# Q from an already turned x, small operations in PSUM, and x turned by DMA before a quantized feed-forward, on one core

## The reference

```python
x = x + xattn(layernorm(x), ctx, ctx, wq, wk, wv, wo)
x = x + ffn(layernorm(x), W_in, b_in, W_out, b_out)
# xattn, 16 heads of 16 features:
corr = irfft(rfft(Q) * conj(rfft(K)))        # along the 128 positions, for each feature
top_vals, top_idx = top_k(corr, 4)
w = softmax(top_vals)
out = sum_i w_i * (V rolled by top_idx_i inside its head)   # then @ wo
# ffn, 1024 hidden features, everything rounded to integers first:
x_q = round(x * 32767 / max|x|);  W_q = round(W * 127 / max|W|)   # one maximum over all of x
hidden = gelu(x_q @ W_in_q + b_in)
out = round(hidden * 32767 / max|hidden|) @ W_out_q + b_out
```

## Time and profile before

| | us |
|---|---|
| three runs | 1146.45, 1155.86, 1157.97; median 1155.86 |
| the profiled execution | 1159.13, its span 1157.3 |
| stage A, to the first L540 matmul | 673 |
| stage B, to the first L570 matmul | 230 |
| stage C | 255 |

### The profile page before, as it was taken

How to read it: one execution, slowest core, us unless ns; L and a number is a source line. 1 busy time by engine, 2 the same in 40 slices (tenths; PEclk the granted TensorE clock), 3 DMA queues, 4 the chain that set the end, 5 groups by cost and what they waited for, 6 DMA issues and landing times.

```text
span 1157.3 us, 30382 instructions
## 1 busy us (share of the span) xinstructions
PE 1088.5 (94%) x9547; PEld 820.8 (71%) x9547; DVE 1091.5 (94%) x3011; ACT 872.0 (75%) x1446; POOL 525.3 (45%) x920
## 2 busy tenths in 40 slices
PE   5889999999999999999999779999999899999998
PEld 4678888788778888888888434444444688888886
DVE  4999999999999999999999779999998899999998
ACT  4567777777677777777777468888888888888885
POOL 3688788888777788788888430000000000000000
PEclk9999999999999999999999789999999899999999
DMA  6222222222222222222221125555557899999995
GB/s 233 64 74 84 83 83 84 83 84 83 73 76 83 74 84 84 84 83 84 83 84 50 40 113 218 230 232 237 224 217 293 324 336 335 339 335 332 338 338 202
DMA packets 67994, 190.50 MB, mean 165 GB/s; under 512 B 6832, under 2 KB 26672, under 8 KB 63792
## 3 DMA queue, kind: packets, MB, share of 16 engines
q1 hardware_dynamic: 66800, 188.13, 44.4%
q10 hardware_dynamic: 1088, 1.05, 0.3%
HBM read 105.27 MB, written 83.89 MB: 163 GB/s over the span
## 4 chain that ended last, share of the span: by engine, by line
DVE 48%; PE 27%; issue 19%; DVEq 1%; SPq 1%; ACT 1%; POOL 1%; DMA 0%; POOLq 0%; ACTq 0%
PE bank L540 19%; DVE arena L1173 7%; DVE arena L978 5%; DVE arena L1036 5%; DVE arena L1188 4%; DVE arena L1029 4%; DVE arena L994 3%; DVE arena L1008 3%; DVE arena L1166 3%; DVE arena L927 3%; DVE arena L941 2%; DVE arena L1001 2%; DVE arena L953 2%; PE bank L404 1%; DVE arena L935 1%
## 5 line engine op out<-in xcount | busy, mean ns | idle before, releaser
L590 ACT ACTIVATE arena<-bank 128x512 f16<-128x512 f32 (+1 forms) x256 | 151.4, 592 | 179.3 <-PE bank L392 158.4
L570 PE MATMUL bank<-wout,arena 128*128 128x256 f16 x2048 | 239.6, 274 | 4.8 <-DVE arena L1166 3.0
L570 PEld LDWEIGHTS bank<-wout,arena 128*128 128x128 f16 x2048 | 196.4, 98 | 49.5 <-DVE arena L1173 16.8
L540 PE MATMUL bank<-store_x,win 128*128 (+1 forms) x1024 | 223.6, 382 | 2.9 <-DVE store_x L1117 2.9
L540 PEld LDWEIGHTS bank<-store_x,win 128*128 128x128 f16 x1024 | 100.5, 98 | 125.9 <-issue 5.7
L1173 DVE SCALAR_TENSOR_TENSOR arena<-arena,wout_rel 128x512 f16<-128x512 int16 x256 | 183.0, 746 | 2.1 <-ACT arena L743 1.0
L700 ACT ACTIVATE arena<-bank,b_in_sb,z_scale 128x512 f32<-128x512 f32 x192 | 147.4, 778 | 15.7 <-PE bank L540 10.3
L601 ACT ACTIVATE arena<-arena 128x256 f32<-128x256 f32 x256 | 140.2, 606 | 5.5 <-POOL arena L778 5.5
L736 ACT ACTIVATE arena<-arena,one 128x1536 int16<-128x1536 f32 x64 | 100.7, 1575 | 36.9 <-DVE arena L1173 33.9
L404 PE MATMUL bank<-store_x,arena 128*128 128x256 f16 x768 | 96.2, 276 | 28.6 <-POOL arena L805 28.5
L404 PEld LDWEIGHTS bank<-store_x,arena 128*128 128x128 f16 x768 | 70.4, 98 | 62.8 <-POOL arena L805 41.3
(11 more groups left out here) (115 smaller groups left out, 2175.0 us busy)
## 6 DMA issues: line engine op xcount, KB each, us to landing
hidden_scratch<-arena SPq DMA_DIRECT2D x32, 1536.0 KB, 5.1
arena<-hidden_scratch SPq DMA_DIRECT2D x64, 768.0 KB, 7.0
arena<-in_x SPq DMA_DIRECT2D x64, 256.0 KB, 3.1
arena<-in_ctx_turned SPq DMA_DIRECT2D x64, 256.0 KB, 2.7
x_scratch<-arena SPq DMA_DIRECT2D x64, 256.0 KB, 2.0
arena<-x_scratch SPq DMA_DIRECT2D x32, 512.0 KB, 6.1
out<-arena SPq DMA_DIRECT2D x32, 512.0 KB, 3.8
store_x<-in_L_ffn_W_in SPq DMA_DIRECT2D x1, 1024.0 KB, 8.1
```

The source lines that it names most:

```text
L540: last = nc.tensor.matmul(bank[b][:, :], win16[:, c, f * P:(f + 1) * P], rhs_of(c), start=s == 0 and c == 0, stop=s == 1 and c == DC - 1)
L570: last = nc.tensor.matmul(bank[m * 2 + k // 2][:, k % 2 * D:(k % 2 + 1) * D], gbuf[:, s, f, k * P:(k + 1) * P], wout16[:, f, :], start=f = ...
L590: nc.scalar.activation(dst, src, ACT.Copy).then_inc(S[done], 1)
```

## The change

Stage A. x comes a second time from memory, turned. Its Q projection no longer waits for layernorm: wq is centred once (the mean of its rows is subtracted, mean_of_wq and center_wq), the turned x is split (high_xt, low_xt) and projected (project_q), ACT scales the result by the power of the variance (take_q_scaled), and dft_q transforms it. dft_norm, low_fx, the first normalization on ACT and turn_ln2 are gone. K and Q projections share PSUM bank 1, V and the mixed output share bank 7, and bank 2 now holds the small operands of the mixing weights (hot, head_dim_i, rsum, rsum_of). The mask multiplication goes from POOL to DVE, one DVE transpose of 128 partitions makes all blocks, and ACT copies the four diagonal ones into mt (spread_blocks). The two power chains of POOL are one (scale_both). The feed-forward weights are handled in pieces: maxima on DVE in steps 6 to 15, scaling and rounding on ACT in steps 12 to 15 and 20 to 23, and one DMA transpose lays W_in out at SP step 20. Their loads and those of the biases move from the start into steps 2 to 4. All `step` orders are new.

Stage B. The second layernorm's result is stored as it is. Quads 0 and 1 are turned by PE at the end of stage A (turn_early, take_early); quads 2 to 31 are rounded and split in the old layout and turned by a DMA transpose of 128 x 2048 float16 (turn_x), one for each quad, on SP's queue between the stores. One of four loads of stage C is issued later.

Stage C. Chunk 6 of the high halves moves from DVE to ACT.

```diff
--- before.py
+++ after.py
@@ -26,9 +26,11 @@
 EPS = 1e-5
 SAVED = 6
 PARTS_OF_F = ((0, 3), (3, 6), (6, 8))
-HIGH_ON_ACT = (1, 3, 5, 7)
+HIGH_ON_ACT = (1, 3, 5, 6, 7)
 FINISH_AFTER = {4: 0, 6: 1}
-SCALE_STEP = 3
+W_STEP = 6
+AHEAD = 5
+EARLY_BANK = (1, 3, 4, 1)
 
 
...
+        hot = bank[2][:, 0:2 * P].rearrange("p (g r k) -> p g r k", g=4, r=HD)
+        small = lambda a, n: bank[2][:, 2 * P + a:2 * P + a + n].rearrange("p (g k) -> p g k", g=4)
+        head_dim_i = small(0, 16).bitcast(I32)
+        rsum = small(16, 4)
+        rsum_of = small(20, 8)
...
+            def load_x_turned(p):
+                wait(sp, S["xt_ready"], p)
+                sp.dma_start(xturn, x_turned[p]).then_inc(s_xt_in, 16)
...
+                    load_x_turned(t)
+                if active(t, 5):
+                    store_x1(t - 5)
+                if t == 2:
+                    sp.dma_start(w_in_raw, w_in.rearrange("(c p) d -> p c d", p=P)).then_inc(S["w_in_loaded"], 16)
+                if t == 3:
+                    sp.dma_start(w_out_raw, w_out.rearrange("(c p) n -> p c n", p=P)).then_inc(S["w_out_in"], 16)
+                if t == 4:
+                    sp.dma_start(b_in_sb[:, :], b_in.rearrange("(c p) -> p c", p=P), allow_slow_non_contiguous=True).then_inc(S["b_in_in"], 16)
+                    sp.dma_start(b_out_sb[:, :], b_out.rearrange("(a n) -> a n", a=1).broadcast_to([P, D])).then_inc(S["b_out_in"], 16)
+                if t == W_STEP + 14:
+                    sp.wait_ge(S["w_in_staged"], FC // 2)
+                    sp.dma_start_transpose(win16.rearrange("p f c n -> p (f c) n"), w_in_q.rearrange("p c d -> p (c d)")).then_inc(s_win, 16)
...
+            def turn_x(q):
+                sp.wait_ge(S["xlo_done"], q + 1)
+                wait(sp, S["b_mm"], (q - 2) * FC)
+                sp.dma_start_transpose(xt[q % 3].rearrange("p s n c t -> p (s n c) t"), xq[:, q].rearrange("p s k -> p (s k)")).then_inc(s_xt[q % 3], 16)
+
+            sp.wait_ge(s_win, 16)
+            for q in range(QUADS - 2):
+                turn_x(q + 2)
+                store_hidden(q, q % 2)
...
+            def mean_of_wq():
+
+                pe.wait_ge(S["center"], 1)
+                pe.wait_ge(s_w_in[0], 16)
                 for c in range(DC):
-                    for b in range(2):
-                        last = nc.tensor.matmul(freq(2)[:, c, :, b, :], xn[:, b, c * P:(c + 1) * P], dft, start=True, stop=True)
-                last.then_inc(S["front_fx"], 1)
+                    last = nc.tensor.matmul(bank[4][:, 0:D], minus_mean, w_attn_raw[:, 0, c, :], start=c == 0, stop=c == DC - 1)
+                last.then_inc(S["w_mean"], 1)
...
+            def project_q(p):
+
+                if p == 0:
+                    pe.wait_ge(S["w_split"], 2)
+                pe.wait_ge(S["xt_ready"], p + 1)
+                wait(pe, S["kf_out"], upto(p + 1))
+                for b in range(2):
+                    for c in range(DC):
+                        for k, (i, j) in enumerate(PARTS):
+                            last = nc.tensor.matmul(bank[1][:, b * D:(b + 1) * D], xt16[:, i, c, b * P:(b + 1) * P], w16[:, j, 0, c, :],
+                                                    start=c == 0 and k == 0, stop=c == DC - 1 and k == 2)
+                last.then_inc(S["qp_done"], 1)
...
+            def dft_q(p):
+
+                pe.wait_ge(S["qf_out"], p + 1)
                 if p == 0:
...
+                    for b in range(2):
+                        last = nc.tensor.matmul(bank[4][b * NF:(b + 1) * NF, r * D:(r + 1) * D], dft[:, r * NF:(r + 1) * NF], qf[:, b, :],
+                                                start=True, stop=True)
                 last.then_inc(S["q_done"], 1)
...
-            def turn_ln2(p):
-
-                pe.wait_ge(S["xn1_done"], p + 1)
-                wait(pe, S["xnt_out"], p)
-                wait(pe, S["ot_out"], upto(p + 3))
-                for c in range(DC):
-                    for b in range(2):
-                        last = nc.tensor.transpose(four(7)[:, c, b, :], xn1[:, b, c * P:(c + 1) * P], ident)
-                last.then_inc(S["xnt_done"], 1)
...
+            def turn_early(n):
+
+                pe.wait_ge(S["xn1_done"], n + 1)
+                pe.wait_ge(S[("qf_out", "terms_done", "q_out", "early_out")[n]], 1 if n == 3 else PAIRS)
+                if n == 0:
+                    pe.wait_ge(S["kf_out"], PAIRS)
+                for b in range(2):
+                    for c in range(DC):
+                        last = nc.tensor.transpose(bank[EARLY_BANK[n]][:, (b * DC + c) * P:(b * DC + c + 1) * P], xnt[:, n, b, c * P:(c + 1) * P], ident)
+                last.then_inc(S["turned_early"], 1)
+
...
+            def take_q_scaled(p):
+                act.wait_ge(S["qp_done"], p + 1)
+                act.wait_ge(S["scales_done"], p + 1)
                 wait(act, S["q_done"], p)
-                copy(fx16[:, 0].rearrange("p c r k -> p (c r k)"), bank[2][:, :], "fx_out")
+                for b in range(2):
+                    last = nc.scalar.activation(qf[:, b, :], pair(1)[:, b, :], ACT.Copy, scale=rs[(p + AHEAD) % 2][:, 1, b, :])
+                last.then_inc(S["qf_out"], 1)
...
+            def spread_blocks(p):
+                if p == 0:
+                    act.wait_ge(S["mt_zero"], 1)
+                act.wait_ge(S["bt_done"], p + 1)
+                wait(act, S["ot_done"], p)
+                for i in range(4):
+                    part = slice(32 * i, 32 * i + 32)
+                    last = nc.scalar.activation(mt.rearrange("p c b l -> p (c b) l")[part, :, part], blocks[part], ACT.Copy)
+                last.then_inc(S["mt_out"], 1)
+
...
+                if t == PAIRS + 5:
+                    for n in range(4):
+                        take_early(n)
...
                 high(q, 5)
+                high(q, 6)
                 high(q, 7)
...
+                ln1 = 0 <= p + AHEAD < PAIRS
+                ln2 = 0 <= p < PAIRS
+                if not ln1 and not ln2:
+                    return
+                a, b, m = 0 if ln2 else 1, 2 if ln1 else 1, p % 2
+                if ln1:
+                    pool.wait_ge(S["ln1_stats"], p + AHEAD + 1)
...
+                    nc.gpsimd.tensor_scalar(nm[m], mv[m][:, 0, :, 0:1], -1.0, None, ALU.mult)
+                nc.gpsimd.tensor_scalar(rs[m][:, a:b], mv[m][:, a:b, :, 1:2], EPS, None, ALU.add).then_inc(S["ln_pow"], 1)
+                pow_count[0] += 1
+                pool.wait_ge(S["ln_pow"], pow_count[0])
+                last = nc.gpsimd.tensor_tensor(rs[m][:, a:b], rs[m][:, a:b], half[:, a:b], ALU.pow)
+                if ln2:
+                    last.then_inc(S["ln_pow"], 1)
+                    pow_count[0] += 1
+                    pool.wait_ge(S["ln_pow"], pow_count[0])
+                    last = nc.gpsimd.tensor_tensor(nm[m], nm[m], rs[m][:, 0], ALU.mult)
+                last.then_inc(S["scales_done"], 1)
...
+            def low_xt(p):
+                pool.wait_ge(S["xt_high"], p + 1)
+                nc.gpsimd.tensor_tensor(xt16[:, 1], xturn, xt16[:, 0], ALU.subtract).then_inc(S["xt_ready"], 1)
...
+            def center_wq():
+
+                dve.wait_ge(S["w_mean"], 1)
+                V.tensor_tensor(w_attn_raw[:, 0], w_attn_raw[:, 0], bank[4][:, 0:D].unsqueeze(1).broadcast_to([P, DC, D]), ALU.add).then_inc(S["w_centred"], 1)
...
+            def spread_weights(p):
+                dve.wait_ge(S["wsum_done"], p + 1)
+                dve.wait_ge(S["rsum_done"], p + 1)
+                wait(dve, S["bt_done"], p)
+                V.tensor_tensor(wmask, wmix.unsqueeze(2).broadcast_to([P, 4, 2, HD]), rsum_of.unsqueeze(3).broadcast_to([P, 4, 2, HD]),
+                                ALU.mult).then_inc(S["w2_done"], 1)
+
             def turn_weights(p):
 
-                if p == 0:
-                    dve.wait_ge(S["mt_zero"], 1)
                 dve.wait_ge(S["w2_done"], p + 1)
-                wait(dve, S["ot_done"], p)
-                for i in range(4):
-                    part = slice(32 * i, 32 * i + 32)
-                    last = V.transpose(mt.rearrange("p c b l -> p (c b) l")[part, :, part], wmask.rearrange("p g j r -> p g (j r)")[part])
-                last.then_inc(S["mt_out"], 1)
-
-            def low_fx(p):
-
-                dve.wait_ge(S["fx_out"], p + 1)
-                V.tensor_tensor(fx16[:, 1].rearrange("p c r k -> p (c r k)"), bank[2][:, :],
-                                fx16[:, 0].rearrange("p c r k -> p (c r k)"), ALU.subtract).then_inc(S["fx_low"], 1)
+                wait(dve, S["mt_out"], p)
+                V.transpose(blocks.rearrange("p g k -> p (g k)"), wmask.rearrange("p g j r -> p (g j r)")).then_inc(S["bt_done"], 1)
...
+            def weights(t):
...
+                if 0 <= n < 4:
+                    largest_w(w_in_raw, win_max, n)
+                if n == 4:
+                    scales(win_max, win_up).then_inc(S["w_in_scaled"], 1)
+                if 5 <= n < 9:
```

(14 more changed lines are left out.)

511 lines of the change are left out of this document (235 added, 276 removed).

## The result

The changed kernel takes 1096.97 us, the median of 4 runs (1095.57 to 1097.34); the kernel before took 1156.07 beside it (1146.45 to 1157.97). The ratio is 0.951 with a 95% interval of 0.946 to 0.956, so it is 59 us faster, and the forecast of 1105 is 8 us too high.

A forecast was written before the change was run, and what follows sets the result against it. DVE was taken to bound stage A (9.79 us per step) and lead C, PE to bound B. Gains 40.7 + 3 + 2 + 0 + 5 = 51 us; 1155.9 - 51 = 1105 us, 8 in 10 range 1083 to 1155.

The forecast's parts named there:

- the head: Start of stage A, project_q of pair 0 to pair 8: 79.7 us before, a gain of 2.8, say 3 us.
- the tail: End of stage A after pair 63: loses the last turn and copy, gains four turns of early pairs; gain 2 us.
- stage C: One of DVE's four L1166 per quad goes to ACT, DMA takes part back: 0.16 x 32 = 5 us gained.
- the forecast's own range: Whole kernel: a stage A step of 8.8 to 9.4 us, head, tail and C +-6: 1086 to 1128 us; chance 0.62.
- Stage A, per step: Steps from pair 8 to 63: 9.05 us instead of 9.79, PE the new bound, a gain of 40.7 us.
- 8 steps of 9.3 are 74.4: Head of stage A: the first 8 steps take 9.3 us each, 74.4 us, instead of 79.7.
- bias loads: Head of stage A: moved to step 4, they may hold SP 4.82 us against 2.6 of slack; 2.5 us added.
- Stage B: 30 DMA transposes of 512 KB, 2.5 us each, hidden behind PE with 3.1 us left per quad: cost 0.
- Rival 3: Stage B: a transpose's 16 blocks go one after the other, 22.6 us each; 471 us more, about 1575; chance 0.07.
- Rival 1: Stage A: ACT's fixed order of waits or the exponent's chain holds a step at 9.6 or more; 1136 us; chance 0.16.
- Rival 2: Stage B: the DMA transpose becomes the bound, costing 30 x (X - 3.1) us from X = 3.1 on; chance 0.15.
- Rival 4: Stage A: PSUM operands don't free DVE, or a second collision replaces L961; DVE 8.5 us, time as forecast; no chance given.

The follow-up runs named there:

- first experiment: The changed kernel with the transform of K (dft_k, 8 matmuls) issued twice in each step of stage A: 1148.99 us.
- experiment on the loads: The changed kernel with the loads of both feed-forward weights and both biases issued ahead of the first step, as before the change: 1096.69 us.
- the experiment: The kernel before without the rounding of w_in and w_out on DVE, filled with a constant instead: 1151.17 and 1161.24 us in two runs.
- second experiment: The changed kernel with the K and V projections made of two of their three float16 parts, 8 fewer matmuls per step: 1055.91 us.

## Why the prediction was right, and where it was not

The total came nearer than its terms. The stretches of the profiled execution add up to 62.5 us where the forecast had 51. That execution of the kernel before was 3 us above the median, and the gain of the head, forecast 13 us too low, was partly offset by those of the tail (1.9 too high) and of stage C (1.2 too high). The ends of the forecast's own range, -14 and +19 us with 6 more each way, are 1085 and 1130, not 1086 and 1128.

**Stage A, per step: right.** 9.00 us against 9.05, since dft_q takes 0.97 from start to start, between its two ends of 0.89 and 1.02. PE is the bound (first experiment), and DVE's, ACT's and POOL's loads came out within 0.1 us of the values taken, or inside the range for ACT. The text counts ACT's lost operations wrongly, as four of 256 and two of 512 elements; they are two and two, and the 2.4 us stand. Two small sizes were off and hidden: L1041 takes 0.154, and the power on four numbers takes 1.04 us, not 0.71. The weight pieces filled ACT and DVE and still cost PE 1.8 us in five steps between pairs 11 and 17 (9.1 to 9.9 us), for which the sum had nothing; that this and the 0.05 us per step nearly cancel over the 55 steps is luck.

**The head: the failed step.** The term "8 steps of 9.3 are 74.4", plus 2.5 for the bias loads, was 13 us too high. The measured head is 27.6 us for the first four steps (6.1 to 7.7 each, by the starts 17.40 and 45.01) and 36.0 for four of 9.00. I gave PE a full step's work from pair 0 on, though in the first steps the later stages of the pipeline have no pair yet: 4 x 9.3 - 27.6 = 9.6 us of the 13. PE is busy without a gap in these short steps too (25.00 of 25.00 us from 20 to 45 us), so it has less work there and does not wait. The bound of 9.05 belongs to full steps only; the four behind them took 9.00 and not 9.3, another 1.2. The loads' 2.5 are the next part, and they don't exist (experiment on the loads). Before, DVE was full from pair 2 on, and the large weight operations stood in it at most of their length: the roundings for about 5.4 us of their 7.0 (the experiment), the maxima and scales of w_out for 3.3 by the timeline (argued only).

**The tail: 0.1 instead of 2.** The last turn that is gone was not on the path. In the kernel before it ran beside the maximum of the last pair, and the reduction over all pairs had to follow both:

```profile
668.54 0.69 DVE L1022 TENSOR_REDUCE xmax<-arena 128x1 f32<-128x512 f32 x1 [2.81 <-ACT arena L601]
```

```profile
668.56 1.12 PE L479 MATMUL bank<-cst,arena 128*128 128x128 f32 x4 [4.12 <-ACT arena L601]
669.47 0.63 PE L382 MATMUL bank<-cst,one 128*128 128x128 f32 x2
```

Both were released by the same normalization, and the maximum (0.69, then 0.22 for the reduction) ended when the turn's time from start to start was over. I had costed a removed operation without looking at what ran beside it. This is read from rows; no run tests it.

**Stage B: right.** 2.5 us of engine time, below a free 3.1. The Trainium skill (DMA: Bandwidth & Descriptors, Latency and other measured facts) has 261 GB/s for a transpose with a non-contiguous middle dimension and about 350 to 400 for a contiguous one, an estimated 2.0 and 1.3 to 1.5 us; the prediction named the first alone. The share of the DMA engines gives 2.5, 512 KB at 210 GB/s, and the measurement decides. Rival 3 is out: 16 blocks land in 3.7 us together, where the 1309 ns of the Trainium skill (VectorE: DVE Perf Modes, The three transpose paths), taken 16 times over, made an estimated 20.9.

**Stage C: right in direction, with a wrong reason for the discount.** A quad gained 0.12 us of the 0.26 that left DVE, where the forecast had 0.16, and DMA is not what kept the rest; DVE is still busy 98.9% of C. DVE's rows at the same place of two consecutive quads, and ACT's beside them, show it:

```profile
939.94 0.75 DVE L1259 SCALAR_TENSOR_TENSOR arena<-bank,one,arena 128x512 f32<-128x512 f32 x1
940.69 1.41 DVE L1244 SCALAR_TENSOR_TENSOR arena<-arena,wout_rel 128x512 f16<-128x512 int16 x2
...
947.57 0.75 DVE L1259 SCALAR_TENSOR_TENSOR arena<-bank,one,arena 128x512 f32<-128x512 f32 x1
948.41 0.75 DVE L1244 SCALAR_TENSOR_TENSOR arena<-arena,wout_rel 128x512 f16<-128x512 int16 x1
```

```profile
939.96 1.93 ACT L813 ACTIVATE arena<-arena,wout_rel 128x512 f16<-128x512 int16 x3
...
947.68 1.32 ACT L813 ACTIVATE arena<-arena,wout_rel 128x512 f16<-128x512 int16 x2
```

L1259's successor normally starts 0.66 us after it. Here it starts 0.75 and 0.84 after it, at 940.69 and 948.41, just as the first of ACT's L813 (0.706 us each) ends, at 940.67 and 948.39. DVE now waits there once per quad for a half that ACT makes, 0.09 and 0.18 us, on average the missing 0.14; I tried no kernel that takes this wait away, so it is read from rows and not shown by a run.

**The rivals.** Rival 1 did not occur with PE's full work per step, but most of the eleven long steps of the second experiment are its mechanism: it begins where the weight pieces are more than what DVE and ACT have left. Rival 2 sits at X = 2.5, below its threshold of 3.1, which is worked out. Rival 4 is confirmed in part: without the PSUM placement the steady steps keep 9.0 us, as forecast, and the weight steps lose 5 us, which was not.
